# Graph attention and a mixture of experts: one half's rows stored as two half-precision parts and turned by DMA instead of by TensorE

## The reference

```python
def _L0_gnn_ref(query, key, value, adj_matrix, Wq, bq, Wk, bk, Wv, bv, Wm, bm):
    q = query @ Wq.T + bq
    k = key @ Wk.T + bk
    v = value @ Wv.T + bv
    scores = jnp.einsum('nd,md->nm', q, k) / q.shape[0] ** 0.5
    adj_scores = scores * adj_matrix
    adj_scores = jnp.where(jnp.abs(adj_scores) < 1e-05, -1000000000.0, adj_scores)
    prob = jax.nn.softmax(adj_scores, axis=-1)
    x = jnp.einsum('nm,md->nd', prob, v)
    return x @ Wm.T + bm

def _L0_ffn_ref(x, Wg, bg, We, be):
    gate = jax.nn.softmax(x @ Wg + bg, axis=-1)
    topk_vals, topk_idx = jax.lax.top_k(gate, 2)
    # the two gates of a row, divided by their sum; zero for the other six experts
    y = jnp.einsum('bsi,eoi->bseo', x, We) + be
    return jnp.einsum('bseo,bse->bso', y, gate_sparse)

x = x + _L0_gnn_ref(_layernorm(x), key, value, adj, ...)
x = x + _L0_ffn_ref(_layernorm(x)[None], Wg, bg, We, be)[0]
```

## Time and profile before

| | us |
|---|---|
| median of 3 runs | 1810.99 |
| lowest, highest | 1809.45, 1811.38 |
| the profiled execution, its own time | 1809.39 |
| its span, first to last instruction | 1807.6 |
| TensorE busy (share of the span) | 1781.9 (99%) |
| VectorE busy | 1200.8 (66%) |
| ScalarE busy | 743.8 (41%) |
| GpSimd busy | 244.7 (14%) |

### The profile page before, as it was taken

The page is one execution under the profiler, slowest core; times in us unless marked ns, Lnnn a source line. Parts: engine busy times, 40 slices in busy tenths (PEclk is TensorE's granted clock), DMA queues, the critical chain, the costliest instruction groups (busy, mean ns, idle before and its releaser), DMA issues.

```text
span 1807.6 us, 33030 instructions
## 1 busy us (share of the span) xinstructions
PE 1781.9 (99%) x8770; PEld 839.2 (46%) x8770; DVE 1200.8 (66%) x3200; ACT 743.8 (41%) x1445; POOL 244.7 (14%) x285
## 2 busy tenths in 40 slices
PE   8999999999999999999999999999999999999997
PEld 4554444444444444444444444444444444455553
DVE  7888766666666666666676766666666666465443
ACT  4444444444444344344444333333334444234333
POOL 2000000100000000000010000000000100245654
PEclk9999999999999999999999999999999999999999
DMA  6555455777767676666676666565555568999986
GB/s 210 173 188 188 154 134 138 162 168 170 160 166 167 163 167 158 162 166 153 163 168 143 166 150 147 136 140 139 134 135 138 132 146 197 233 286 240 189 153 83
DMA packets 428620, 296.64 MB, mean 164 GB/s; under 512 B 319249, under 2 KB 335633, under 8 KB 428562
## 3 DMA queue, kind: packets, MB, share of 16 engines
q1 hardware_dynamic: 390962, 232.45, 52.1%
q0 software_dynamic: 16864, 38.35, 10.9%
q10 hardware_dynamic: 20736, 25.18, 4.7%
HBM read 152.68 MB, written 67.72 MB: 122 GB/s over the span
## 4 chain that ended last, share of the span: by engine, by line
PE 90%; issue 3%; DVE 3%; POOL 1%; DMA 1%; SPq 1%; ACT 1%; DVEq 0%; POOLq 0%; ACTq 0%
PE ps L1477 17%; PE ps L1479 17%; PE ps L1478 17%; PE ps L1590 12%; PE ps L1592 12%; PE ps L1591 12%; PE ps L1662 1%; PE ps L1534 1%; DMA out<-val_region,tok_ids 1%; DVE work L1429 1%; POOL out L716 0%; SPq L496 0%; DVE work L1421 0%; PE ps L1600 0%; DVEq L1425 0%
## 5 line engine op out<-in xcount | busy, mean ns | idle before, releaser
L1477 PE MATMUL ps<-key_region,work 128*128 128x512 f16 (+1 forms) x1336 | 506.4, 379 | 2.5 <-issue 1.3
L1478 PE MATMUL ps<-key_region,work 128*128 128x512 f16 (+1 forms) x1336 | 506.3, 379 | 0.0
L1479 PE MATMUL ps<-key_region,work 128*128 128x512 f16 (+1 forms) x1336 | 506.3, 379 | 0.0
L795 ACT ACTIVATE work<-work 128x512 f32<-128x512 f32 x256 | 161.2, 630 | 566.7 <-DVE work L1098 564.7
L1590 PE MATMUL ps<-val_region,work 128*128 128x512 f16 x1024 | 387.8, 379 | 2.2 <-DVE work L1140 2.2
L1592 PE MATMUL ps<-val_region,work 128*128 128x512 f16 x1024 | 388.0, 379 | 0.0
L1591 PE MATMUL ps<-val_region,work 128*128 128x512 f16 x1024 | 388.0, 379 | 0.0
L1098 DVE SCALAR_TENSOR_TENSOR work<-ps,r_cur,work 128x512 f32<-128x512 f32 x256 | 191.8, 749 | 147.6 <-PE ps L1479 133.6
L1120 DVE TENSOR_TENSOR work<-work 128x512 f16<-128x512 f32 x256 | 176.3, 690 | 71.3 <-ACT work L808 70.0
L1108 DVE CUSTOM_DVE_ANT_0 work<-work 128x512 f32<-128x512 f32 x256 | 177.3, 693 | 49.5 <-DVE work L1105 49.3
L803 ACT ACTIVATE work<-work,exp_bias 128x512 f32<-128x512 f32 x256 | 181.4, 709 | 64.4 <-DVE exp_bias L1116 54.6
(11 more groups left out here) (202 smaller groups left out, 1594.7 us busy)
## 6 DMA issues: line engine op xcount, KB each, us to landing
work<-in_adj SPq DMA_DIRECT2D x256, 256.0 KB, 2.9
val_region<-slots SPq DMA_DIRECT2D x58, 257.0 KB
work<-in_valueT SPq DMA_DIRECT2D x8, 1024.0 KB, 6.7
work<-in_x SPq DMA_DIRECT2D x8, 1024.0 KB, 5.4
work<-in_keyT SPq DMA_DIRECT2D x8, 1024.0 KB, 5.4
q_scratch<-work SPq DMA_DIRECT2D x8, 1024.0 KB, 5.1
work<-q_scratch SPq DMA_DIRECT2D x32, 256.0 KB, 2.7
work<-in_x SPq DMA_DIRECT2D x32, 256.0 KB, 3.0
```

The costliest lines, as they stand in the source:

```text
L795: nc.scalar.activation(w[:, c * CW:(c + 1) * CW], s_adj[:, c % 2, :], ACT.Abs).then_inc(abs_done, 1)
L1477: nc.tensor.matmul(bank, st[0], mv[0], start=(k == 0), stop=False)
L1478: nc.tensor.matmul(bank, st[0], mv[1], start=False, stop=False)
L1479: last = nc.tensor.matmul(bank, st[1], mv[0], start=False, stop=(k == n - 1))
```

## The change

The first half's rows are kept as float16 parts. `row_pack` is a new tile of 514 words, in whose first 512 words ScalarE and VectorE write the high and the low half of a row; it is what POOL now scatters for half 0, with number and gate behind it. `row_split`, which was a tile of its own and is read by `turn_rows`, is now this tile's front part.

In iterations t = 20 to 30, SP issues for three blocks of half 0 each (33 in all, `TURNED`) a transposing transfer from `slots[0]` in DRAM into the tile `stage` (`turn_block`) and a plain transfer from there to `tok_dram` in DRAM (`keep_block`). `stage` has one buffer, which each transfer waits for. The first stands behind the first two probability chunks, the second behind `turn_rows`, the third between the last probability chunk and `q_in`.

In the experts' stage a block of half 0 is loaded turned: the first 33 by a plain transfer of 2 KB for each partition from `tok_dram`, the other six by a transposing transfer straight from `slots[0]`, and all with a second transfer of two words for each row (number and gate). TensorE multiplies straight out of `tok_in`. For half 0 there are no transposes on TensorE, no high copy on ScalarE and no low part on VectorE. The loads of blocks 0 to 2 move ahead, between the last tile's probability chunks. The order becomes 33 of half 0, 33 of half 1, six pairs. The table steps of half 0 in iteration 19 are spread over more places.

Cut to its core:

```diff
-    LEAD, PAIRS = 29, 10
+    LEAD, PAIRS = 33, 6
+    AT_ONCE = 3
...
+        row_pack = carve(ROW)
+        row_split = row_pack[:, 0:D].bitcast(F16)
...
+        stage = q1_words.bitcast(F16).rearrange("p (f n) -> p f n", f=2 * KC)
...
-            def attend_io(t, h=None, last=False):
+            def turn_block(t, i):
+
+                b = (t - (TH + 4)) * AT_ONCE + i
+                sp.wait_ge(overlaps_done, 1)
+                sp.wait_ge(padded[0], 16 * E)
+                sp.wait_ge(slotted, 32 * TH)
+                if not is0(b):
+                    sp.wait_ge(rows_kept, b * 16)
+                settle()
+                at = sp.value_load(tab_row[0:1, bass.ds(b, 1)], min_val=0, max_val=DUMMY * P)
+                sp.dma_start_transpose(stage, slots[0].bitcast(F16)[bass.ds(at, P), 0:2 * D]).then_inc(rows_turned, 16)
+
+            def keep_block(t, i):
+
+                b = (t - (TH + 4)) * AT_ONCE + i
+                sp.wait_ge(rows_turned, b * 16 + 16)
+                settle()
+                sp.dma_start(tok_dram[b], stage.rearrange("p f n -> p (f n)")).then_inc(rows_kept, 16)
+
+            def attend_io(t, h=None, last=False, turns=False):
 
                 turn_probs(t - 1, 0)
                 turn_probs(t - 1, 1)
+                if turns:
+                    turn_block(t, 0)
                 adjacency(t, 4)
                 adjacency(t, 5)
                 turn_probs(t - 1, 2)
                 adjacency(t, 6)
+                if turns:
+                    keep_block(t, 0)
                 turn_probs(t - 1, 3)
...
                     if c == 4 and h is not None:
                         turn_rows(t - 2)
+                    if turns and c in (4, 7):
+                        turn_block(t, 1 + c // 7)
+                    if turns and c == 6:
+                        keep_block(t, 1)
                 if not last:
                     sp.wait_ge(s_mm, t * C + C)
                     settle()
                     sp.dma_start(q_in, q_dram[t + 1]).then_inc(q_loaded, 16)
                     adjacency(t + 1, C - 1 - ADJ)
+                if turns:
+                    keep_block(t, 2)
...
+            def load_block(st):
+                if st.has(TOKS):
+                    user = steps[st.first - TOKS]
+                    if user.h:
+                        sp.wait_ge(tokT_mm, user.i1 + 1)
+                    else:
+                        sp.wait_ge(y_mm, user.count())
+                    sp.wait_ge(tok_meta, user.count())
...
+                else:
+                    at = sp.value_load(tab_row[0:1, bass.ds(st.at, 1)], min_val=0, max_val=DUMMY * P)
+                    sp.dma_start(row[:, 0:D].bitcast(F16), tok_dram[st.at]).then_inc(tok_loaded[st.b16], 16)
+                    sp.dma_start(row[:, D:ROW], slots[0][bass.ds(at, P), D:ROW]).then_inc(tok_loaded[st.b16], 16)
...
             for c in range(5):
                 turn_probs(T - 1, c)
                 load_bias(c)
+                if 0 < c < 4:
+                    if c == 1:
+                        sp.wait_ge(rows_kept, 16 * TURNED)
+                    load_block(lead[c - 1])
...
             def turn_block(st):
-                pe.wait_ge(tok_loaded[st.b16], st.uses(TOKS) * 16)
-                if st.has(2):
-                    pe.wait_ge(tokT_lo, st.count(2))
+                if not st.h:
+                    return
...
             def multiply_block(st):
...
-                pe.wait_ge(tokT_lo, st.count())
+                if st.h:
+                    pe.wait_ge(tokT_lo, st.i1 + 1)
+                    rows = tokT[:, st.t4]
+                else:
+                    pe.wait_ge(tok_loaded[st.b16], st.loads())
+                    rows = turned_row(st).rearrange("p (h k) n -> p h k n", h=2)
```

More of the change, by code:

```diff
@@ L145, in graph_attention_moe_kernel @@
         row_buf = carve(ROW)
+        carve(-taken[0] % 8)
+        row_pack = carve(ROW)
+        carve(-taken[0] % 8)
+        row_split = row_pack[:, 0:D].bitcast(F16)
+        row_hi_part, row_lo_part = row_split[:, 0:D], row_split[:, D:2 * D]
         q1_words = carve(KC * P)
@@ L168, in graph_attention_moe_kernel @@
         y_out = moe_words[:, 0:RING * D].rearrange("p (b d) -> p b d", b=RING)
-        tok_in = [work[:, at:at + ROW] for at in range(12288, 12288 + YB * ROW, ROW)]
-        tok_in += [moe_words[:, at:at + ROW] for at in range(RING * D, RING * D + (TOKS - YB) * ROW, ROW)]
-        row_last = moe_words[:, RING * D + (TOKS - YB) * ROW:RING * D + (TOKS - YB + 1) * ROW]
-        assert len(tok_in) == TOKS and 12288 + YB * ROW <= 14848
+        adj_at = 2 * N
+        tok_in = [work[:, at:at + ROW] for at in (adj_at, adj_at + ROW_AT, adj_at + 2 * ROW_AT, 12288)]
+        tok_in += [moe_words[:, at:at + ROW] for at in range(RING * D, RING * D + (TOKS - YB) * ROW_AT, ROW_AT)]
+        row_last = moe_words[:, RING * D + (TOKS - YB) * ROW_AT:RING * D + (TOKS - YB) * ROW_AT + ROW]
+        assert len(tok_in) == TOKS and adj_at + 3 * ROW_AT <= adj_at + ADJ * CW <= 12288
         ident = sb("ident", [P, P], F32)
@@ L394, in __init__ @@
                 self.at = OF_HALF[:first].count(self.h) + self.h * BLOCKS
+                self.i1 = OF_HALF[:first].count(1)
+                self.t2, self.t4 = self.i1 % 2, self.i1 % YB
                 self.b2, self.bank, self.b8, self.b16 = first % 2, first % YB, first % RING, first % TOKS
@@ L403, in uses, with loads, step_of_row @@
                 return (self.first - back) // n + 1
+            def loads(self):
+                return sum(16 * (2 - OF_HALF[s]) for s in range(self.b16, self.first + 1, TOKS))
+            def step_of_row(self, back):
+                return [s for s in range(SEQ) if OF_HALF[s] == 1][self.i1 - back]
             def added(self, back):
@@ L553, in load_bias @@
                 sp.dma_start(be_all[:, e, :], be[e:e + 1, :].to_broadcast([P, D])).then_inc(we_loaded[e], 16)
+            sp.wait_ge(padded[0], 16 * E)
+            for b in range(RING):
+                sp.wait_ge(y_added[b], PRIMED)
+            sp.wait_ge(slotted, 32 * TH)
+            sp.wait_ge(s_read, T * C)
+            sp.wait_ge(tables_done, 1)
             for c in range(5):
@@ L563, in _ @@
             turn_rows(T - 2)
-            def load_block(st):
-                if st.has(TOKS):
-                    sp.wait_ge(tokT_mm, st.count(TOKS))
-                    sp.wait_ge(tok_meta, st.count(TOKS))
-                at = sp.value_load(tab_row[0:1, bass.ds(st.at, 1)], min_val=0, max_val=DUMMY * P)
-                sp.dma_start(tok_in[st.b16], slots[st.h][bass.ds(at, P), :]).then_inc(tok_loaded[st.b16], 16)
             def expert_ready(e):
@@ L575, in expert_ready @@
                 sp.sem_inc(we_ready, 1)
-            sp.wait_ge(padded[0], 16 * E)
-            for b in range(RING):
-                sp.wait_ge(y_added[b], PRIMED)
-            sp.wait_ge(slotted, 32 * TH)
             sp.wait_ge(bias_done, T)
@@ L583, in _ @@
             sp.wait_ge(p_lo, T * C)
-            sp.wait_ge(tables_done, 1)
-            for st in lead[:YB]:
-                load_block(st)
+            load_block(lead[3])
             expert_ready(0)
@@ L609, in _ @@
             expert_ready(5)
-            for st in lead[21:23]:
-                load_block(st)
+            load_block(lead[21])
             expert_ready(6)
-            load_block(lead[23])
+            load_block(lead[22])
             expert_ready(7)
-            for st in lead[24:]:
+            for st in lead[23:]:
                 load_block(st)
@@ L677, in scatter_row @@
                 settle()
-                row = row_at(t)
+                row = row_at(t) if h else row_pack
                 gates, where = (gate_last, slots_last) if isl(t, T) else (gate, slots_u)
@@ L869, in attend @@
                 if routes:
-                    split_rows(t - 2)
+                    split_rows(t - 2, stores)
                 absolute(t, 4)
@@ L1169, in route_low @@
                 row = row_at(t)
-                nc.vector.tensor_copy(row[:, D:D + 1], row_ids[:, bass.ds(t - h * TH, 1)])
+                nc.vector.tensor_copy((row if h else row_pack)[:, D:D + 1], row_ids[:, bass.ds(t - h * TH, 1)])
                 nc.vector.tensor_tensor(row_lo_part, row[:, 0:D], row_hi_part,
@@ L1413, in block_lo @@
             def block_lo(st):
[L1415 removed]
+                dve.wait_ge(tok_loaded[st.b16], st.loads())
                 if st.has(TOKS):
```

75 lines of the change are left out of this document (50 added, 25 removed).

## The result

| | runs | median us | lowest, highest |
|---|---|---|---|
| before | 13 | 1811.97 | 1809.38, 1815.25 |
| changed | 13 | 1804.40 | 1795.89, 1815.50 |

The ratio is 0.996, with a 95% interval of 0.9943 to 0.9976. The change makes the kernel faster, but by 0.4% and not by the 1.1% of the forecast: 7.6 us of the 19.9 foreseen. Its executions also spread over 20 us where those of before spread over 6. The profiled one took 1799.04 us.

A forecast was written before the change was run, and what follows sets the result against it. TensorE, busy for 1781.9 of 1807.6 us, was taken as the bound; transposes -17.0, start -1.9, VectorE's gaps -3.0 and adds +2 summed to -19.9 us, so 1791.1 us against the median of 1810.99, range 1786 to 1807.

The follow-up runs named there:

- late_loads: The changed kernel with the loads of blocks 0 to 2 moved back behind the last tile's probability chunks; 1802.58 us.
- after_third: The changed kernel run a third time, no edit; 1802.63 us.
- after_again: The changed kernel run once more, no edit, for a second profile; 1805.13 us.
- small_weights: The changed kernel loading only 64 of the 2048 elements per partition in each weight transfer of experts 3 to 7 (outputs not the reference's); 1793.82 us.
- turn_behind_q: The changed kernel with the third turned block of an iteration moved behind the queries instead of ahead of them; 1804.50 us.
- late_and_spread: Changed kernel, weights of experts 3 to 7 loaded behind later blocks, weight waits on ScalarE, block 0 to 2 loads behind the last tile's probability chunks; 1794.24 us.

## What to carry to other kernels

A faster consumer shortens the cover of every transfer that must land meanwhile: before counting time taken off the bound engine, list what its DMA queues have under way in the stretch that gets shorter, how long a load takes to land there, and from which moment each buffer is really free. Spread bulk loads over the time until they are needed instead of issuing them as early as buffers allow. Take the cover of each of a row of transfers, not of the last one. And measure by the starts of the same instruction in both kernels: idle times and busy shares hid 1.1 us of queries and 2.9 us of clock here.

## What the hardware did that I had not expected

TensorE's clock. In a kernel in which it is busy for 98% of the time, a wait of 3.2 us was followed by a stretch of 5 us with a granted clock of 0.52 (nearly all of it at the level of 1.2 GHz), then 0.80; a wait of 8.6 us in late_loads by 0.50 and 0.88. The first of the latter two:

```profile
1585.00:1590.00 5.00, 4.41 (x17) 1.65 (x14) 0.06 (x1) 0.00 (x0) 1.56 (x1) 0.50 1.08 358
```

So a stall of 3.2 us cost 2.9 us of clock besides. It is no fixed price: one of 3.3 us in after_third was followed by 0.77 and 0.89, some 1.7 us, and one of 2.5 us at 1592.08 by 1.7 us. Waits of 2.3 to 2.4 us for the same chunk in after_again, small_weights and turn_behind_q were followed by 1.00, and so was late_and_spread's longest, of 1.3 us. The clock goes with the scatter of the executions: among those of the changed kernel a mean clock of 0.997 stands beside 1795.89 us and one of 0.992 beside 1815.50.

An issue can hold its queue. SP's issues of small transfers, 0.34 us in the iterations, took up to 4.3 us (after_again) while the weights moved, and a transposing one 7.4 instead of 1.26. A queue that waits for no semaphore can thus be late all the same: in after_again these issues stand ahead of the `expert_ready` for which TensorE waited 3.8 us.
